# Experts' silu written with Tanh, the router's sigmoid with Exp and a reciprocal

## The chip, the cores and the metric

The kernel runs on one core of a Trainium2 chip. The metric is the device time of one execution in microseconds (us); several runs are made and their median is compared. The core has TensorE (PE, matmuls; its weight loads are shown as PEld), VectorE (DVE), ScalarE (ACT), GpSimd (POOL) and SyncE (SP, which issues the DMAs). Every engine runs its own instructions in order and waits for the others by semaphores.

## What is computed

A decoder of two layers: six sublayers in a row on 512 tokens of width 256, each followed by a residual addition and a layer norm. The change lies in the sixth, a mixture of 64 experts with a shared expert:

```python
N, TOPK, E, CAP, H, HS = 512, 6, 64, 128, 32, 64
y_s, g_s = split(x @ w_shared_up)                    # 512 x 64 each
shared = (silu(g_s) * y_s) @ w_shared_down
scores = sigmoid(x @ w_gate)                         # 512 x 64
topk_idx = top_k(scores, 6)
w = scores at topk_idx, divided by their sum
# an expert takes at most CAP tokens: valid = position in its list < CAP
g_r, v_r = split(x @ w_up[e])                        # for each expert, 32 each
out_r = (silu(g_r) * v_r) @ w_down[e]
x = layernorm(x + shared + sum over the 6 experts of w * valid * out_r)
```

## The kernel before

The program has six stages, one for each sublayer; each engine's part of stage n is a function `stageN` in that engine's block, with the instructions and the semaphores written out by hand. No scheduler reorders them: what is written is the order on the engine.

Stage 6 doesn't gather tokens by expert. It computes every expert for all 512 tokens and multiplies by a gate that is zero where the expert wasn't chosen. Four experts make a group, so that the hidden units of a group fill 128 partitions, and the 512 tokens lie along the free dimension; there are 16 groups, g = 0 to 15. All data here are float32.

On TensorE (L1124 to L1179): the router's matmuls go to PSUM bank 7. `up(g)` multiplies the tokens by the two halves of a group's up weights, into bank g % 2 (the half that goes through silu) and bank 2 + g % 2; it waits until `gate(g-2)` on VectorE has read these banks. `down(g)` multiplies `hidden` of a group by its down weights and adds to the output in banks 6 and 7. The order is: router, `up(0)` to `up(3)`, the count of tokens per expert (L1148), `up(4)`, the transposes of the gates (L1154), the shared expert's up matmul, `up(5)`, then `down(0)`, the shared expert's down matmuls (L1177), `up(6)`, `down(1)`, `up(7)` and so on to `down(9)`, `up(15)`, and `down(10)` to `down(15)` without anything between them. The matmuls of `up` have line L762, those of `down` L1162.

On ScalarE (L728 to L747): the sigmoid of the router's scores (L730), the silu of each group (`silu_of`, L737) from PSUM to SBUF, a copy of the transposed gates (L742), the silu of the shared expert (L745).

On VectorE (L1577 to L1625): top 8 and their indices (L1581, L1584), the one-hot counts of each of four blocks of tokens (L1596 to L1598), with `gate(0)` behind the first block and `gate(1)` behind the third, then `gate(2)`, `gate(3)`, the capacity test (L1608), `gate(4)`, the shared expert's product (L1611), `gate(5)`, and the loop. `gate(g)` (L1593) multiplies silu by the other half of `up`, from PSUM to the SBUF tile `gated`; `hidden` (L1622) multiplies `gated` by the rows of gates that a DMA has spread over the partitions. In the loop each `hidden(g)` is followed by `gate(g+5)` while there are groups left, so `gate(15)` stands between `hidden(10)` and `hidden(11)`. `link` makes the engine wait for the end of the instruction that it is given before the next one begins.

Of the kernel before, what the change touches and what calls it, by code (L numbers as in the profile page):

```python
# [17 lines left out]
ACT = mybir.ActivationFunctionType  # L18
# [12 lines left out]
N = B * S  # L31
TT = N // P
# [14 lines left out]
E1, HE, HS, TOPK, CAP = 64, 32, 64, 6, 128  # L47
# [18 lines left out]
def build(nc, t, out):  # L66

    with ExitStack() as ctx:
# [5 lines left out]
        def sem(name):  # L74
            if name not in sems:
                sems[name] = ctx.enter_context(nc.semaphore(name))
            return sems[name]
# [3 lines left out]
        def bank(k, n=1):  # L81
            return ps[:, 512 * k:512 * (k + n)]
# [48 lines left out]
        def carve(where, at, shape, dt=F32, rows=P):  # L131

            words = math.prod(shape) * mybir.dt.size(dt) // 4
            assert at + words <= area[where].shape[1], (where, at, shape)
            v = area[where][0:rows, at:at + words]
            if dt != F32:
                v = v.bitcast(dt)
            if len(shape) == 2:
                v = v.rearrange("p (a b) -> p a b", a=shape[0])
            if len(shape) == 3:  # L140
                v = v.rearrange("p (a b c) -> p a b c", a=shape[0], b=shape[1])
            return v

        def tiny(shape, dt=F32):
            v = carve("small", taken["small"], shape, dt)
            taken["small"] += (math.prod(shape) * mybir.dt.size(dt) + 3) // 4
            return v
# [88 lines left out]
        gate1T = carve("b", 0, [N], rows=E1)  # L236
        silu = carve("b", N, [2, N])
# [5 lines left out]
        score1 = carve("b", 8 * N, [TT, E1])  # L243
# [4 lines left out]

        base = 8 * N + 4 * TT * E1 + TOPK * E1
        silu_shared = carve("b", base + N, [N], rows=HS)  # L250
        top1, idx1, idx1f = tiny([TT, 8]), tiny([TT, 8], U32), tiny([TT, 8])
        sum1, rsum1 = tiny([TT]), tiny([TT])

# [58 lines left out]
        def linker(eng, name):  # L312

            count = [0]

            def link(ins):
                count[0] += 1
                ins.then_inc(sem(name), 1)
                eng.wait_ge(sem(name), count[0])
            return link  # L320
# [245 lines left out]
        def _(act):  # L566
            link = linker(act, "act_chain")
# [159 lines left out]

            def stage6():  # L728
                act.wait_ge(sem("score1_ps"), 1)
                act.activation(score1.rearrange("p i e -> p (i e)"), bank(7)[:, 0:TT * E1], ACT.Sigmoid).then_inc(sem("score1_ready"), 1)  # L730

                def silu_of(g):
                    act.wait_ge(sem("up_ps"), g + 1)
                    if g >= 2:

                        act.wait_ge(sem("gated_ready"), g - 1)
                    act.activation(silu[:, g % 2, :], bank(g % 2), ACT.Silu).then_inc(sem("silu_ready"), 1)  # L737

                for g in range(4):
                    silu_of(g)  # L740
                act.wait_ge(sem("gate1T_ps"), 1)
                act.activation(gate1T, bank(5)[0:E1, :], ACT.Copy).then_inc(sem("gate1T_ready"), 1)  # L742
                silu_of(4)
                act.wait_ge(sem("shared_ps"), 1)
                act.activation(silu_shared, bank(4)[HS:2 * HS, :], ACT.Silu).then_inc(sem("silu_shared_ready"), 1)  # L745
                for g in range(5, NG):
                    silu_of(g)  # L747

# [441 lines left out]
        def _(dve):  # L1190
            link = linker(dve, "dve_chain")
            TS, TTN, STT = dve.tensor_scalar, dve.tensor_tensor, dve.scalar_tensor_tensor
# [61 lines left out]
            for c in range(DC):  # L1254
# [10 lines left out]
                if c:  # L1265
# [4 lines left out]
                    op1=ALU.add).then_inc(sem("phi_ready"), 1)  # L1270
# [305 lines left out]

            def stage6():  # L1577
                dve.wait_ge(sem("score1_ready"), 1)
                ids = iota_row[:, 0:E1].unsqueeze(1).broadcast_to([P, TOPK, E1])
                for i in range(TT):  # L1580
                    last = dve.max(top1[:, i, :], score1[:, i, :])  # L1581
                link(last)
                for i in range(TT):
                    last = dve.max_index(idx1[:, i, :], top1[:, i, :], score1[:, i, :])  # L1584
                link(last)
                link(dve.tensor_copy(idx1f, idx1))
                link(dve.tensor_reduce(sum1, top1[:, :, 0:TOPK], AX.X, ALU.add))
                link(dve.reciprocal(rsum1, sum1))

                def gate(g):  # L1590

                    dve.wait_ge(sem("silu_ready"), g + 1)
                    TTN(out=gated[:, g % AHEAD, :], in0=bank(2 + g % 2), in1=silu[:, g % 2, :], op=ALU.mult).then_inc(sem("gated_ready"), 1)  # L1593

                for i in range(TT):
                    link(TTN(out=hot, in0=idx1f[:, i, 0:TOPK].unsqueeze(2).broadcast_to([P, TOPK, E1]), in1=ids, op=ALU.is_equal))  # L1596
                    link(dve.tensor_reduce(picked[:, i, :], hot.rearrange("p k e -> p e k"), AX.X, ALU.add))
                    dve.tensor_copy(picked_b[:, i, :], picked[:, i, :]).then_inc(sem("picked_ready"), 1)  # L1598
                    if i % 2 == 0:
                        gate(i // 2)  # L1600
                link(TTN(out=gate1, in0=picked, in1=score1, op=ALU.mult))
                link(TTN(out=gate1, in0=gate1, in1=rsum1.unsqueeze(2).broadcast_to([P, TT, E1]), op=ALU.mult))
                gate(2)
                gate(3)
                dve.wait_ge(sem("count_ps"), 1)

                flat = gate1.rearrange("p i e -> p (i e)")
                STT(out=flat, in0=bank(6)[:, 0:TT * E1], scalar=float(CAP), in1=flat, op0=ALU.is_le, op1=ALU.mult).then_inc(sem("gate1_ready"), 1)  # L1608
                gate(4)
                dve.wait_ge(sem("silu_shared_ready"), 1)  # L1610
                TTN(out=shared, in0=bank(4)[0:HS, :], in1=silu_shared, op=ALU.mult).then_inc(sem("shared_ready"), 1)  # L1611
                gate(5)
                dve.wait_ge(sem("gated_ready"), AHEAD)
                for g in range(NG):
                    s = g % 2
                    if g >= AHEAD:
                        dve.wait_ge(sem("gated_ready"), g + 1)
                    if g >= 2:

                        dve.wait_ge(sem("hidden_used"), g - 1)  # L1620
                    dve.wait_ge(sem(f"gate_rows_{g % 4}"), 16 * (g // 4 + 1))
                    TTN(out=hidden[:, s, :], in0=gate_rows[:, g % 4, :], in1=gated[:, g % AHEAD, :], op=ALU.mult).then_inc(sem("hidden_ready"), 1)  # L1622
                    if g and g - 1 + AHEAD < NG:
                        dve.wait_ge(sem("hidden_ready"), g)
                        gate(g - 1 + AHEAD)  # L1625
# [52 lines left out]
```

## Time and profile before

| | before |
|---|---|
| time, median of 3 runs | 472.29 us (471.53 to 473.58) |
| span of the profiled execution | 473.8 us |
| TensorE busy | 388.1 us, 82% of the span |
| VectorE busy | 303.7 us, 64% |
| ScalarE busy | 215.5 us, 45% |
| GpSimd busy | 118.4 us, 25% |
| chain of waits, share of the span | TensorE 53%, VectorE 15%, DMA 12%, ScalarE 10% |

The span goes from the first to the last instruction of one execution that was profiled; that execution's time apart from its span isn't given, and the span is 1.5 us above the median of the three runs, which were timed without a profile. The busy shares are means over the six stages, of which only the last, from about 369 us on, is touched by the change. The chain of waits is followed back from the last instruction: at each step to what released it.

### The profile page before, as it was taken

The page shows a single profiled execution, that of the slowest core. Times are in us where ns is not written, and L with a number is a line of the kernel's source. Part 1 is how long each engine was busy: PE and PEld are TensorE (multiplying, and loading weights), DVE is VectorE, ACT ScalarE, POOL GpSimd, SP SyncE. Part 2 cuts the span into 40 slices and gives each one's busy share as a digit, 9 for nine tenths or more (in the row PEclk, how much of TensorE's full clock was granted, in tenths as well). Part 3 has the DMA queues.
Part 4 walks back from the last instruction along what each step waited for, and adds up shares of the span by engine and source line. Part 5 has one row for each costly group of instructions (what it writes and reads, how often), then busy time and mean ns, then how long its engine had stood idle before and what let it go on. Part 6 is the DMA issues. An engine that isn't in the chain of part 4 may idle for free.

```text
span 473.8 us, 6810 instructions
## 1 busy us (share of the span) xinstructions
PE 388.1 (82%) x2387; PEld 225.7 (48%) x2387; DVE 303.7 (64%) x611; ACT 215.5 (45%) x551; POOL 118.4 (25%) x215
## 2 busy tenths in 40 slices
PE   5996969389987999999754867768676998999993
PEld 2645457244434566576532223333344544665572
DVE  4984498959624697878646979989871362132235
ACT  2664221272235765855214789899881311111100
POOL 8248646828460000000080111212110000000002
PEclk9989895779988899999985589998975698999997
DMA  8992110670000000000000999999982004011211
GB/s 244 318 361 25 1 2 1 223 310 1 0 1 0 1 3 0 2 1 1 2 0 13 265 169 172 155 163 173 131 162 51 0 0 143 24 44 49 63 44 44
DMA packets 75521, 39.84 MB, mean 84 GB/s; under 512 B 64160, under 2 KB 71264, under 8 KB 75040
## 3 DMA queue, kind: packets, MB, share of 16 engines
q1 hardware_dynamic: 73184, 39.35, 34.1%
q0 software_dynamic: 2304, 0.07, 1.4%
q8 instruction: 19, 0.31, 0.3%
q14 instruction: 14, 0.11, 0.1%
HBM read 21.58 MB, written 2.88 MB: 52 GB/s over the span
## 4 chain that ended last, share of the span: by engine, by line
PE 53%; DVE 15%; DMA 12%; ACT 10%; issue 5%; POOL 4%; SPq 0%; POOLq 0%; ACTq 0%; DVEq 0%
PE ps L762 27%; ACT area_b L692 7%; PE ps L1162 6%; DMA area_b<-area_b 6%; PE ps L945 5%; PE ps L956 5%; PE ps L975 3%; DMA area_a<-area_b 3%; POOL deltas L490 2%; PE ps L939 2%; DMA area_b<-deltas 1%; DVE area_a L1275 1%; DMA deltas<-entry_w,small 1%; ACT area_a L673 1%; DVE stats L1282 1%
## 5 line engine op out<-in xcount | busy, mean ns | idle before, releaser
L1535 DVE CUSTOM_DVE_ANT_0 area_a<-ps,zero,small 128x1024 f32<-128x1024 f32 x64 | 79.4, 1278 | 9.7 <-ACT area_b L692 5.0
L692 ACT ACTIVATE area_b<-area_a,small 128x1024 int16<-128x1024 f32 x64 | 73.0, 1142 | 11.3 <-DMA area_b<-area_b 5.9
L673 ACT ACTIVATE area_a<-ps,small 128x256 f32<-128x256 f32 (+1 forms) x128 | 51.9, 432 | 31.0 <-DVE small L1426 28.7
L459 POOL TENSOR_SCALAR var_eps<-meanvar 128x1 f32<-128x1 f32 x24 | 6.6, 273 | 225.3 <-DVE meanvar L1283 225.2
L762 PE MATMUL ps<-xT_odd,early 128*128 128x512 f32 x128 | 59.5, 613 | 0.0
L1054 PE MATMUL ps<-area_b 128*128 128x512 bf16 x128 | 45.0, 446 | 13.5 <-DVE small L1535 12.4
L1593 DVE TENSOR_TENSOR area_b<-ps,area_b 128x512 f32<-128x512 f32 x16 | 11.1, 691 | 55.7 <-ACT area_b L737 55.7
L1426 DVE TENSOR_REDUCE small<-ps 128x4 f32<-128x1024 f32 (+1 forms) x24 | 29.3, 1222 | 18.3 <-PE ps L945 18.1
L737 ACT ACTIVATE area_b<-ps 128x512 f32<-128x512 f32 x16 | 9.5, 596 | 67.2 <-PE ps L762 67.2
L762 PE MATMUL ps<-area_b,xT_even 128*128 128x512 f32 x64 | 31.1, 631 | 9.0 <-ACT area_b L650 9.0
L762 PEld LDWEIGHTS ps<-xT_odd,early 128*128 128x128 f32 x128 | 25.0, 197 | 27.1 <-issue 26.6
L547 POOL TENSOR_SCALAR small<-small 128x1 f32<-128x1 f32 x64 | 12.5, 195 | 87.5 <-DVE small L1535 87.5
L1162 PE MATMUL ps<-area_a,area_b 128*128 128x256 f32 x128 | 31.0, 392 | 2.6 <-DVE area_b L1622 2.6
L1435 DVE COPY area_b<-ps 128x512 f32<-128x512 f32 x48 | 30.8, 681 | 1.0 <-PE ps L956 0.9
L1162 PEld LDWEIGHTS ps<-area_a,area_b 128*128 128x128 f32 x128 | 24.8, 195 | 11.5 <-issue 7.8
L490 POOL DMA_INDIRECT deltas<-entry_w,small x16 | 26.0, 1624 | 10.6 <-DMA deltas<-entry_w,small 3.8
L945 PE MATMUL ps<-area_a,area_b 32*128 32x256 f32 (+1 forms) x160 | 28.1, 460 | 0.0
L956 PE MATMUL ps<-ident,area_a 128*128 128x128 f32 x192 | 27.2, 286 | 1.0 <-DVE area_b L1435 1.0
L673 ACT ACTIVATION_READ_ACCUMULATOR area_a<-ps,small 128x1 f32 x128 | 27.9, 218 | 0.0
L956 PEld LDWEIGHTS ps<-ident,area_a 128*128 128x128 f32 x192 | 21.3, 144 | 12.2 <-ACT area_a L673 8.5
L1054 PEld LDWEIGHTS ps<-area_b 128*128 128x128 bf16 x128 | 8.2, 102 | 34.3 <-DVE small L1535 28.6
L762 PEld LDWEIGHTS ps<-area_b,xT_even 128*128 128x128 f32 x64 | 12.3, 203 | 22.0 <-issue 22.0
(265 smaller groups left out, 667.4 us busy)
## 6 DMA issues: line engine op xcount, KB each, us to landing
early<-in_w_up_dram SPq DMA_DIRECT2D x1, 4096.0 KB, 16.1
area_b<-gates_out SPq DMA_DIRECT2D x16, 256.0 KB, 3.0
deltas<-area_b SPq DMA_DIRECT2D x1, 2112.0 KB, 17.8
area_b<-deltas SPq DMA_DIRECT2D x2, 1024.0 KB, 5.9
area_a<-in_w_down_dram SPq DMA_DIRECT2D x1, 2048.0 KB, 8.5
early<-in_ctxT_dram SPq DMA_DIRECT2D x1, 1024.0 KB, 13.1
early<-in_ctx_dram SPq DMA_DIRECT2D x1, 1024.0 KB, 14.0
early<-in_w_qkv_dram SPq DMA_DIRECT2D x2, 384.0 KB, 5.1
```

The costliest lines, as they stand in the source:

```text
L490: pool.indirect_dma_start(out=deltas, out_offset=bass.IndirectOffsetOnAxis(ap=place[:, j:j + 1], axis=0), in_=entry_w[:, j, :], in_offset= ...
L673: a = act.activation(p1[:, n % 2, x * nk * P:(x + 1) * nk * P], scores1(n)[:, x * nk * P:(x + 1) * nk * P], ACT.Exp, bias=nmx1[:, n % 2, x ...
L692: act.activation(px[:, u % PX, :], sx[:, u % 3, :], ACT.Exp, bias=nbx[:, u:u + 1], accum_out=zx[:, i, h:h + 1]).then_inc(sem("px_ready"), 1)
L762: mm = pe.matmul(dst, lhsT(c), rhs(c), start=start and c == 0, stop=stop and c == DC - 1, **kw)
L945: mm = pe.matmul(dst, qT1[rows, c, i * P:(i + 1) * P], kT1[rows, c, heads, kt * P:(kt + 1) * P], start=False, stop=b == nk - 1)
L956: mm = pe.transpose(bank(4 + x)[:, y * P:(y + 1) * P], p1[:, n % 2, (4 * x + y) * P:(4 * x + y + 1) * P], ident[:])
L975: mm = pe.matmul(bank(6)[g * HU * DH1:(g + 1) * HU * DH1, c * P:(c + 1) * P], v1[:, (kt * (H1 // HU) + c * UC + g) * HU + j, :], pT1[:, n ...
L1054: mm = pe.matmul(bank(2 * (u % 2) + half), qTx[:, h // 2, h % 2, i * P:(i + 1) * P], kTx[:, h // 2, half * 512:(half + 1) * 512], start=Tr ...
L1162: mm = pe.matmul(proj(i), hidden[:, g % 2, i * P:(i + 1) * P], w_down[:, g, :], start=g == 0 and i % 2 == 0, stop=g == NG - 1, skip_group_ ...
L1426: dve.tensor_reduce(nmx1[:, n % 2, 0:8 // nk], scores1(n).rearrange("p (h k) -> p h k", k=nk * P), AX.X, ALU.max, negate=True).then_inc(se ...
L1435: dve.tensor_copy(pT1[:, n % 4, 4 * x * P:4 * (x + 1) * P], bank(4 + x)).then_inc(sem("pT1_ready"), 1)
L1535: dve.tensor_tensor_reduce(sx[:, u % 3, :], bank(2 * (u % 2), 2), zero[:].broadcast_to([P, B * M]), qsc[:, i, h:h + 1], LOWEST, ALU.add, A ...
```

## The change

Silu is written as x/2 * (1 + tanh(x/2)): ScalarE computes tanh(x/2) in place of silu, a new scalar_tensor_tensor on VectorE makes (tanh + 1) * x, reading x from PSUM, and the product with the other half follows as before, linked behind it. The factor 1/2 of the groups goes into the copy of the transposed gates. For the shared expert, whose x stands in other partitions than the product, ScalarE makes a copy of x/2 as well, in a new tile `half_shared`. The router's sigmoid becomes 1 / (1 + exp(-x)): Exp on ScalarE, an addition and a reciprocal on VectorE.

```diff
+        half_shared = carve("b", base + 2 * N, [N], rows=HS)
...
             def stage6():            # ScalarE
                 act.wait_ge(sem("score1_ps"), 1)
-                act.activation(score1.rearrange("p i e -> p (i e)"), bank(7)[:, 0:TT * E1], ACT.Sigmoid).then_inc(sem("score1_ready"), 1)
+                act.activation(score1.rearrange("p i e -> p (i e)"), bank(7)[:, 0:TT * E1], ACT.Exp, scale=-1.0).then_inc(sem("score1_ready"), 1)
...
-                    act.activation(silu[:, g % 2, :], bank(g % 2), ACT.Silu).then_inc(sem("silu_ready"), 1)
+                    act.activation(silu[:, g % 2, :], bank(g % 2), ACT.Tanh, scale=0.5).then_inc(sem("silu_ready"), 1)
...
-                act.activation(gate1T, bank(5)[0:E1, :], ACT.Copy).then_inc(sem("gate1T_ready"), 1)
+                act.activation(gate1T, bank(5)[0:E1, :], ACT.Copy, scale=0.5).then_inc(sem("gate1T_ready"), 1)
...
-                act.activation(silu_shared, bank(4)[HS:2 * HS, :], ACT.Silu).then_inc(sem("silu_shared_ready"), 1)
+                act.activation(silu_shared, bank(4)[HS:2 * HS, :], ACT.Tanh, scale=0.5)
+                act.activation(half_shared, bank(4)[HS:2 * HS, :], ACT.Copy, scale=0.5).then_inc(sem("silu_shared_ready"), 1)
...
             def stage6():            # VectorE
                 dve.wait_ge(sem("score1_ready"), 1)
+                link(TS(score1, score1, 1.0, None, ALU.add))
+                link(dve.reciprocal(score1, score1))
...
                     dve.wait_ge(sem("silu_ready"), g + 1)
+                    link(STT(out=silu[:, g % 2, :], in0=silu[:, g % 2, :], scalar=1.0, in1=bank(g % 2), op0=ALU.add, op1=ALU.mult))
                     TTN(out=gated[:, g % AHEAD, :], in0=bank(2 + g % 2), in1=silu[:, g % 2, :], op=ALU.mult).then_inc(sem("gated_ready"), 1)
...
                 dve.wait_ge(sem("silu_shared_ready"), 1)
+                link(STT(out=silu_shared, in0=silu_shared, scalar=1.0, in1=half_shared, op0=ALU.add, op1=ALU.mult))
                 TTN(out=shared, in0=bank(4)[0:HS, :], in1=silu_shared, op=ALU.mult).then_inc(sem("shared_ready"), 1)
```

What the diff doesn't show is that the program loads ScalarE's function tables where a function needs another set. On ScalarE, at the beginning of stage 6, this stood in the program before (`area_b` is the memory in which the tiles of this stage lie, `ps` is PSUM):

```order
L622 ACTIVATE xT_odd<-ps 128x2x128 x4
L730 ACT_TABLE_LOAD
L730 ACTIVATE area_b<-ps 128x256
L737 ACT_TABLE_LOAD
L737 ACTIVATE area_b<-ps 128x512 x4
L742 ACTIVATE area_b<-ps 64x512
```

and this stands there now, one line further down in the file:

```order
L623 ACTIVATE xT_odd<-ps 128x2x128 x4
L731 ACTIVATE area_b<-ps 128x256
L738 ACTIVATE area_b<-ps 128x512 x4
L743 ACTIVATE area_b<-ps 64x512
L738 ACTIVATE area_b<-ps 128x512
L746 ACTIVATE area_b<-ps 64x512
L747 ACTIVATE area_b<-ps 64x512
```

Both loads of stage 6 are gone; the one that is left stands at the beginning of the program, as it did before.

On VectorE, from the capacity test to the first `gate` of the loop, this stood before:

```order
L1608 SCALAR_TENSOR_TENSOR area_b<-ps,area_b 128x256
L1593 TENSOR_TENSOR area_b<-ps,area_b 128x512
L1611 TENSOR_TENSOR area_b<-ps,area_b 64x512
L1593 TENSOR_TENSOR area_b<-ps,area_b 128x512
L1622 TENSOR_TENSOR area_b<-area_b 128x512 x2
```

and this stands there now (L1597 is the new operation, L1598 the product of `gate`, L1628 `hidden`):

```order
L1613 SCALAR_TENSOR_TENSOR area_b<-ps,area_b 128x256
L1597 SCALAR_TENSOR_TENSOR area_b<-area_b,ps 128x512
L1598 TENSOR_TENSOR area_b<-ps,area_b 128x512
L1616 SCALAR_TENSOR_TENSOR area_b<-area_b 64x512
L1617 TENSOR_TENSOR area_b<-ps,area_b 64x512
L1597 SCALAR_TENSOR_TENSOR area_b<-area_b,ps 128x512
L1598 TENSOR_TENSOR area_b<-ps,area_b 128x512
L1628 TENSOR_TENSOR area_b<-area_b 128x512 x2
```

Each `gate` has one operation more, and `hidden(0)`, the first of the last row, stands behind both operations of `gate(5)`. On the other engines the program is the same.

## Rows read from the trace of the kernel before

**Rows 1.** The first line of the profile's page.

```profile
span 473.8 us, 6810 instructions
```

**Rows 2.** Chain of waits in stage 6: start us, length us, what.

```profile
392.26 5.17 PE ps L762 x12
...
455.24 1.74 PE ps L1162 x8
```

**Rows 3.** Stretches: length, busy us of PE, PEld, DVE, ACT, POOL; clock; DMA.

```profile
369.00:397.40 28.40, 28.40 (x81) 14.06 (x80) 13.14 (x36) 7.16 (x11) 0.00 (x0) 0.87 0.05 11
...
405.10:457.00 51.90, 51.86 (x161) 30.31 (x160) 12.63 (x20) 5.97 (x10) 0.00 (x0) 1.00 0.16 46
```

**Rows 4.** Timeline of TensorE, `down(0)`: start, length, engine, line [idle before, releaser].

```profile
399.64 3.21 PE L1162 MATMUL ps<-area_a,area_b 128*128 128x256 f32 x8 [2.23 <-DVE area_b L1622]
```

**Rows 5.** Timeline of VectorE and TensorE at the last `gate`.

```profile
455.97 0.69 DVE L1593 TENSOR_TENSOR area_b<-ps,area_b 128x512 f32<-128x512 f32 x1 [3.87 <-ACT area_b L737]
456.58 1.28 DVE L1622 TENSOR_TENSOR area_b<-area_b 128x512 f32<-128x512 f32 x2
...
457.32 8.90 PE L1162 MATMUL ps<-area_a,area_b 128*128 128x256 f32 x40 [0.35 <-DVE area_b L1622]
```

**Rows 6.** VectorE by line and form: count | busy us, mean ns | idle before.

```profile
L1275 DVE RECIPROCAL area_a<-area_a 128x512 f32<-128x512 f32 x2 | 6.7, 3352 | 0.1
...
L1216 DVE RECIPROCAL area_b<-area_b 128x128 f32<-128x128 f32 x1 | 1.0, 953 | 0.0
...
L1273 DVE TENSOR_SCALAR area_a<-area_a 128x512 f32<-128x512 f32 x2 | 0.9, 426 | 0.1
...
L1608 DVE SCALAR_TENSOR_TENSOR area_b<-ps,area_b 128x256 f32<-128x256 f32 x1 | 0.4, 412 | 0.0
...
L1215 DVE TENSOR_SCALAR area_b<-area_b 128x128 f32<-128x128 f32 x1 | 0.2, 220 | 0.0
```

**Rows 7.** Timeline of VectorE, `gate(0)` to `hidden(0)`.

```profile
378.38 0.69 DVE L1593 TENSOR_TENSOR area_b<-ps,area_b 128x512 f32<-128x512 f32 x1 [2.06 <-ACT area_b L737]
...
382.07 0.68 DVE L1593 TENSOR_TENSOR area_b<-ps,area_b 128x512 f32<-128x512 f32 x1
...
385.31 0.69 DVE L1593 TENSOR_TENSOR area_b<-ps,area_b 128x512 f32<-128x512 f32 x1 [0.23 <-ACT area_b L737]
388.68 0.69 DVE L1593 TENSOR_TENSOR area_b<-ps,area_b 128x512 f32<-128x512 f32 x1 [2.67 <-ACT area_b L737]
...
398.07 0.69 DVE L1593 TENSOR_TENSOR area_b<-ps,area_b 128x512 f32<-128x512 f32 x1 [2.75 <-ACT area_b L737]
398.80 1.29 DVE L1622 TENSOR_TENSOR area_b<-area_b 128x512 f32<-128x512 f32 x2
```

**Rows 8.** Stretches of TensorE alone: length, busy us, granted clock, DMA share, GB/s.

```profile
226.00:235.00 9.00, 6.46 (x95) 1.00 0.01 3
325.00:328.00 3.00, 1.62 (x20) 1.00 0.80 148
328.00:331.00 3.00, 2.71 (x20) 0.59 1.02 193
397.00:400.00 3.00, 0.77 (x3) 1.00 0.94 307
400.00:403.00 3.00, 3.00 (x9) 0.53 0.49 179
```

**Rows 9.** Timeline of weight loads: the first of `up(3)` and of `up(4)`.

```profile
383.99 0.19 PEld L762 LDWEIGHTS ps<-xT_odd,early 128*128 128x128 f32 x1 [0.24 <-issue]
...
388.11 0.30 PEld L762 LDWEIGHTS ps<-xT_odd,early 128*128 128x128 f32 x2
```

**Rows 10.** Timeline of ScalarE at the beginning of stage 6.

```profile
369.17 1.28 ACT L730 ACT_TABLE_LOAD   x1
372.08 0.38 ACT L730 ACTIVATE area_b<-ps 128x256 f32<-128x256 f32 x1 [1.62 <-PE ps L762]
...
377.75 0.60 ACT L737 ACTIVATE area_b<-ps 128x512 f32<-128x512 f32 x1 [3.99 <-PE ps L762]
```

## The prediction

> **What bounds the kernel now.** I read the chain of waits first, for the part of the program that the change touches: stage 6, the experts, which begins near 369 us of a span of 473.8 us [rows 1]. The chain runs through TensorE nearly everywhere there: matmuls of `up` to 397.4 us (392.26 + 5.17), and `down(10)` to 456.98 us (455.24 + 1.74) [rows 2]. The table of stretches says the same: from 369 to 397.4 TensorE is busy 28.40 us of 28.40, from 405.1 to 457 it is busy 51.86 of 51.90, while VectorE works 13.14 and 12.63 us in these stretches [rows 3]. So VectorE has much room on average, and an operation added to it costs nothing where TensorE has other work. The question is only at which places TensorE waits for VectorE, and at which it comes to.
>
> The waits of TensorE in this stage are two. `down(0)` at 399.64 starts after 2.23 us of idleness, released by VectorE's L1622 (`hidden`) [rows 4]: TensorE has done `up(0)` to `up(5)` and has nothing else until `hidden(0)` exists. And `down(11)` at 457.32 starts after 0.35 us, again released by L1622 [rows 5]: there are no more `up` blocks to fill the time. Between these, in the loop, VectorE waits 3.87 us for ScalarE before each `gate` [rows 5], so an operation of under a microsecond disappears.
>
> **The change, step by step.**
>
> *One operation more in each `gate`.* Its operands are 128x512 float32, one in PSUM. No row of before has just this form. The nearest are the `gate` product itself, L1593, 0.69 us, which also reads PSUM at this size [rows 7], and the scalar_tensor_tensor L1608 that reads PSUM at 128x256, 412 ns [rows 6]. I take 0.69 us, the row of the same size. The product behind it now waits for a semaphore of its own engine; a linked pair shows some 0.04 us between end and start (398.07 + 0.69 = 398.76, next start 398.80 [rows 7]). So a `gate` grows by 0.73 us. Bounds: 0.41, if the width cost nothing beyond the 256 row, and 0.86, twice that row and the gap.
>
> *Before `down(0)`.* `gate(5)` starts at 398.07 after 2.75 us of waiting for ScalarE, and `hidden(0)` at 398.80 stands right behind it [rows 7]. Tanh and silu are both one pass of ScalarE, so 398.07 stays. `hidden(0)` moves to 399.53, `down(0)` to 400.37: **0.73 us on the path**. The clock enters here. In 397 to 400 the granted clock is 1.00, in 400 to 403 it is 0.53 [rows 8], that is 2.4 and then 1.2 GHz, after the idle 2.23 us. The 0.36 us and a little more that TensorE did at full clock before the fall would now be done after it. If the rise comes when it came before, the term is about 0.6; if the rise comes as much later, it is about 1.0. I keep 0.73.
>
> *The tail.* `gate(15)` starts at 455.97, and `hidden(11)` at 456.58 queues behind it on VectorE although it doesn't need its result; `down(11)` waits for `hidden(11)` [rows 5]. So another **0.73 us on the path**, and TensorE's idle time grows from 0.35 to 1.08 us.
>
> *The ten `gate`s between them* (`gate(6)` to `gate(14)`, and `gate(4)`, which stands before the shared expert) cost nothing: the cover is the 3.87 us of VectorE's waiting per group, with 3.1 left. Were that cover gone, each group would cost 0.73, some 7 us in all. The shared expert's ScalarE copy (0.6 us, as a 512-wide pass of Silu [rows 10]) and its VectorE operation stand in the 2.75 us ahead of `gate(5)`.
>
> *The router's add and reciprocal*, 128x256, on VectorE ahead of everything else in stage 6. Reciprocals: 953 ns at width 128 and 3352 at 512 [rows 6], a straight line of 6.25 ns an element, so 1.75 us at 256. The add: 220 ns at 128 and 426 at 512 [rows 6], so 0.29. With two links, 2.1 us. Behind them queue the top-8 search, the index search and the first one-hot count. Their cover is the 2.06 us that VectorE idles before `gate(0)` at 378.38 [rows 7]: just enough, so `gate(0)` starts as before. If that cover were gone, they would cost up to 2.1 us.
>
> *`gate(0)` to `gate(3)`, the start.* From here VectorE has no idle time until `gate(2)`. `gate(1)`, at 382.07 before, starts 0.73 later and ends at 384.21 (382.80 + 0.73 + 0.68). `up(3)` writes the banks that `gate(1)` reads; its first weights were loaded at 383.99, with 0.24 us of slack ahead of each load [rows 7, 9]. With the 0.06 us that a semaphore took from `hidden(11)` to `down(11)` (456.58 + 0.68 to 457.32 [rows 5]) the load comes at 384.27, 0.28 late, of which the slack takes 0.24: 0.04 us. `gate(2)`, at 385.31 after 0.23 idle, is pushed by 1.46 - 0.23 = 1.23 and ends at 387.96; `up(4)`'s weights were loaded at 388.11 [rows 7, 9]: in time by a tenth. `gate(3)` waited 2.67 us before 388.68 [rows 7], so there VectorE is back in step; the capacity test L1608 behind it comes 0.73 later, at about 390.5, and the transposes that wait for it follow the eight matmuls of `up(4)`, which end near 391.5 (388.11 and 8 x 0.43). Start: **0.05 us**; bounds 0 (all within the slack) and 0.3 (add at the 512-wide price, three more links).
>
> *Two table loads fewer.* ScalarE's loads for Sigmoid and Silu, 1.28 us each (two; one stands in the rows), are gone. After the first ScalarE still waited 1.62 us for TensorE, before the first Silu 3.99 us [rows 10]. So nothing is gained: ScalarE only waits longer. If these waits were not there, they would be worth 2.57.
>
> **Sum.** 0.73 + 0.73 + 0.05 = 1.51 us; by the bounds 0.8 (two waits of 0.41) to 2.3 (1.0, 0.86 and 0.3, with rounding). The profiled execution spans 473.8 us, already 1.5 above the median of the runs, 472.29, and 0.2 above their highest, so it was one of the slower ones; a profile of the changed kernel should span about 475.3, and its runs have a median of 472.29 + 1.51 = **473.8 us**. 0.5% of 472.29 is 2.4 us, about what a measurement of this kernel can tell from no change; the forecast lies under that.
>
> **The rivals.**
>
> *The clock falls in the tail (slower).* TensorE's idle time between `down(10)` and `down(11)` becomes 1.08 us. Idle time of that order is where the granted clock sometimes falls: in 325 to 328 TensorE was busy 1.62 of 3.00 us, and the clock went from 1.00 there to 0.59 in 328 to 331 [rows 8]. Against it: in 226 to 235 it was busy 6.46 of 9.00, and the clock stayed at 1.00 throughout [rows 8]. [...] The price, from the fall at 400: a stretch of 3.4 us or so at half clock (0.53 over 400 to 403), of which half is lost, 1.7 us. Then 1.5 + 1.7 = 3.2, 475.5 us. Chance 0.11.
>
> *VectorE becomes the bound of the start (slower).* The cover before `gate(0)` is used up to 0.05 us, and `up(3)` has a slack of 0.24. Anything that the router's two operations cost beyond 2.1 us goes to the path. With a reciprocal at the 512-wide price, 3.35, it is 1.6 more: 475.4 us; the decisive point is 1 us more, at 474.8. The two measured widths lie on both sides of the new one, so 0.05.
>
> *Only one wait counts.* The longer idle time ahead of `down(0)` costs nothing, because the stretch at the low clock that follows ends at the same time and the work after the rise catches up. Then 0.8 us, 473.1. Against it: TensorE is busy without a break from 405.1, so nothing is there to catch up with. 0.07.
>
> *The table loads were paid for (faster).* If the switch of tables cost TensorE or VectorE something that the idle times hide, the change gives back 2.57 us and takes 1.51: 471.2 us. What speaks against it is that TensorE's first `up` blocks run straight through 369 to 397.4, whatever ScalarE does. 0.04. The Trainium skill (ScalarE: Activation LUTs, What ACT_TABLE_LOAD costs) speaks for it: it puts a switch of sets at 1283 ns for the load and 1380 ns for draining the engine, 2.66 us in all, and advises calling activations by set, as the changed kernel does. This trace agrees on the load (1.28), and has a draining time in no row: what stands behind the first load, 1.62 us, is ended by TensorE. By that figure two switches would be an estimated 5.3 us, and the sum 468.5.
>
> **How the numbers follow.** The forecast has 0.73, the clock 0.11, the start 0.05, one wait 0.07, the tables 0.04. The predicted time is the forecast's. Its own range, 473.1 to 474.6, with the spread of a median of a few runs (they lie between 471.53 and 473.58) is 472.7 to 475.0; to hold 8 in 10 with cases beyond it, I extend it upward to the clock's case: 472.7 to 475.7. Slower by over 0.5% (above 474.65): the clock 0.11, the start 0.04, the upper edge of the forecast 0.04, together 0.19. Faster by over 0.5%: half of the tables' case and a little for the spread, 0.03. The rest, 0.78, is within 0.5%.
>
> **What would show it.** In the changed profile: the new operation near 0.69 us and the reciprocal near 1.75; `gate(0)`'s first operation at about 378.4; TensorE without idle time up to 397.4; its wait before `down(0)` near 3.0 and before `down(11)` near 1.1, with the granted clock at 1.00 after the latter; no table load in stage 6, and ScalarE waiting for TensorE as before. It is wrong if TensorE waits before `up(2)`, `up(3)` or `up(4)` for more than 0.3 us, if a wait shows up inside the loop, or if the clock falls after 457.

## The result: slower, and by more than forecast

| | before | after |
|---|---|---|
| median, 4 runs each | 472.45 us (471.53 to 473.58) | 477.67 us (476.67 to 479.94) |
| ratio, 95% interval | | 1.0117 (1.0079 to 1.0155) |
| span of the profiled execution | 473.8 us | 476.2 us |
| once more, on one chip: median | 475.36 us (29 runs, 468.19 to 479.19) | 478.26 us (12 runs, 472.29 to 483.97) |
| ratio, 95% interval | | 1.0076 (1.0012 to 1.0139) |

The forecast was 473.8 us in a range of 472.7 to 475.7. The first measurement is above the range, 5.2 us over before. The second, with more runs, is over before by 2.9 us (medians) or 3.6 us (ratio) and shows how far runs of one program lie apart: 11 us for the kernel before. (The ratios are formed without the runs that lie more than 1.5% above the fastest of their kernel, in the second measurement 17 of the 29 before and 3 of the 12 after; the medians are those of all runs.) So the first part of the question is what stage 6 really costs, and the second what the rest of the 5.2 is.

Stage 6 in the profile after. First VectorE's timeline, from the router to the gates (the lines of the file are one to six further down; L1597 is the new operation in `gate`, L1598 the product, L1628 `hidden`); these answer to [rows 5, 7].

```profile
375.09 0.29 DVE L1581 TENSOR_SCALAR area_b<-area_b 128x256 f32<-128x256 f32 x1 [4.50 <-ACT area_b L731]
375.42 1.75 DVE L1582 RECIPROCAL area_b<-area_b 128x256 f32<-128x256 f32 x1
...
380.96 0.68 DVE L1597 SCALAR_TENSOR_TENSOR area_b<-area_b,ps 128x512 f32<-128x512 f32 x1
381.68 0.69 DVE L1598 TENSOR_TENSOR area_b<-ps,area_b 128x512 f32<-128x512 f32 x1
...
386.08 0.69 DVE L1598 TENSOR_TENSOR area_b<-ps,area_b 128x512 f32<-128x512 f32 x1
...
400.59 0.69 DVE L1597 SCALAR_TENSOR_TENSOR area_b<-area_b,ps 128x512 f32<-128x512 f32 x1 [1.55 <-ACT area_b L738]
401.31 0.69 DVE L1598 TENSOR_TENSOR area_b<-ps,area_b 128x512 f32<-128x512 f32 x1
402.03 1.29 DVE L1628 TENSOR_TENSOR area_b<-area_b 128x512 f32<-128x512 f32 x2
```

The prices came as worked out: 0.29 for the add, 1.75 for the reciprocal, 0.68 to 0.69 for the new operation, 0.72 from its start to that of the product. `gate(0)` at 380.96 follows VectorE's work without idle time: the 2.06 us that stood before it [rows 7] are used up, and it starts 10.79 us after the last norm product of stage 5, as before (10.80). TensorE's timeline of the same kernel:

```profile
374.43 12.24 PE L764 MATMUL ps<-xT_odd,early 128*128 128x512 f32 x24
386.82 3.70 PE L764 MATMUL ps<-xT_odd,early 128*128 128x512 f32 x8 [0.16 <-DVE area_b L1598]
...
402.87 1.97 PE L1164 MATMUL ps<-area_a,area_b 128*128 128x256 f32 x8 [2.95 <-DVE area_b L1628]
...
459.63 8.90 PE L1164 MATMUL ps<-area_a,area_b 128*128 128x256 f32 x40 [1.08 <-DVE area_b L1628]
```

The two waits grew as forecast, from 2.23 to 2.95 us [rows 4] and from 0.35 to 1.08 [rows 5], and a new one of 0.16 stands before `up(3)`. None of the waits that the prediction named as signs of being wrong is there: nothing over 0.3 us before `up(2)` to `up(4)`, and nothing inside the loop. ScalarE, with no table load, only waits longer than in [rows 10]:

```profile
374.67 0.38 ACT L731 ACTIVATE area_b<-ps 128x256 f32<-128x256 f32 x1 [2.92 <-PE ps L764]
379.84 0.60 ACT L738 ACTIVATE area_b<-ps 128x512 f32<-128x512 f32 x1 [4.78 <-PE ps L764]
```

And the granted clock of TensorE (stretches: length, busy, clock, DMA):

```profile
370.00:374.00 4.00, 3.36 (x16) 0.50 0.00 0
374.00:378.00 4.00, 4.00 (x8) 0.51 0.00 0
400.00:404.00 4.00, 1.13 (x5) 1.00 0.75 228
404.00:408.00 4.00, 4.00 (x15) 1.00 0.44 131
459.00:467.00 8.00, 7.37 (x34) 1.00 0.12 33
```

Stage 6 began at 1.2 GHz, and after the 2.95 us of idle time the clock did *not* fall, though it fell after 2.23 in the profile before [rows 8]. So the two spans, 473.8 and 476.2, can't be compared directly. For what follows each profile has four numbers: the length of stage 6 (from the start of the last norm product of stage 5 to that of stage 6, 367.58 and 471.28 before, 370.17 and 473.60 after); what the low clock took of it (TensorE's busy time by its granted clock's shortfall from 1.00, added up over quarters of a microsecond); the rest; and TensorE's idle time in it.

The runs x1 to x12 are described below; "filled" ones have extra matmuls that keep TensorE busy ahead of stage 6.

| profile | stage 6 | low clock | rest | TensorE idle |
|---|---|---|---|---|
| before | 103.70 | 5.84 | 97.86 | 8.12 |
| x1 before again | 98.06 | 0.00 | 98.06 | 8.11 |
| after | 103.43 | 3.62 | 99.81 | 9.71 |
| x2 after again | 103.43 | 3.60 | 99.83 | 9.74 |
| x3 functions only | 99.74 | 1.71 | 98.04 | 8.12 |
| x4 VectorE only | 103.43 | 3.24 | 100.19 | 10.10 |
| x5 filled, before | 99.70 | 1.71 | 97.99 | 8.11 |
| x6 filled, after | 103.24 | 1.66 | 101.58 | 11.14 |
| x7 after, Sigmoid | 99.50 | 0.00 | 99.50 | 9.56 |
| x8 after, hidden early | 100.93 | 4.02 | 96.91 | 7.34 |
| x9 filled, after, Sigmoid | 99.51 | 0.00 | 99.51 | 9.57 |
| x10 filled, router only | 98.71 | 0.00 | 98.71 | 8.25 |
| x11 filled, before, hidden early | 96.90 | 0.00 | 96.90 | 7.22 |
| x12 after, Sigmoid, again | 102.59 | 3.12 | 99.47 | 9.56 |

### The profile page after: what moved, and what is told of

The parts are those of the page before. It is cut to its first block and busy times, and to the rows that moved or that the text cites. A ratio compares the mean times of both kernels' runs of the same rounds, so it can differ in the third digit from the quotient of the medians.

```text
span 476.2 us, 6805 instructions
## 1 busy us (share of the span) xinstructions
PE 379.4 (80%) x2364; PEld 222.5 (47%) x2387; DVE 317.3 (67%) x630; ACT 213.3 (45%) x550; POOL 117.7 (25%) x215
## 5 line engine op out<-in xcount | busy, mean ns | idle before, releaser
L1056 PE MATMUL ps<-area_b 128*128 128x512 bf16 x116 | 41.2, 441 | 16.1 <-DVE small L1537 13.3
L1597 DVE SCALAR_TENSOR_TENSOR area_b<-area_b,ps 128x512 f32<-128x512 f32 x16 | 11.0, 686 | 41.3 <-ACT area_b L738 41.3
L1164 PE MATMUL ps<-area_a,area_b 128*128 128x256 f32 x128 | 29.8, 380 | 4.0 <-DVE area_b L1628 4.0
L947 PE MATMUL ps<-area_a,area_b 32*128 32x256 f32 (+1 forms) x160 | 29.3, 477 | 0.0
```

Source lines behind the costliest of these rows:

```text
L947: mm = pe.matmul(dst, qT1[rows, c, i * P:(i + 1) * P], kT1[rows, c, heads, kt * P:(kt + 1) * P], start=False, stop=b == nk - 1)
L1056: mm = pe.matmul(bank(2 * (u % 2) + half), qTx[:, h // 2, h % 2, i * P:(i + 1) * P], kTx[:, h // 2, half * 512:(half + 1) * 512], start=Tr ...
L1164: mm = pe.matmul(proj(i), hidden[:, g % 2, i * P:(i + 1) * P], w_down[:, g, :], start=g == 0 and i % 2 == 0, stop=g == NG - 1, skip_group_ ...
```

## The experiments

Ratios are to runs of the kernel before on the same chip. There were three such groups of 29 runs, one for x1 to x4, one for x5 to x8 and one for x9 to x12; their medians are 475.36, 475.05 and 474.80 us.

### Which part costs: functions or VectorE

x1 and x2 are the two kernels unchanged.

> The kernel before, unchanged, to have the spans and granted clocks of its own runs beside its times, and a second profile. If the profiled execution of before was an outlier (its span of 473.8 us lies above the time of every run), the spans here lie near 470.7, which is 472.4 less the 1.7 that lie between span and time in the runs of the changed kernel. If before has less around its span than the changed kernel has, the spans lie at 472 and above, and part of the 5.2 us stands outside the program's work. Ratio to before 1.000 in either case.

Measured: 473.94 us, ratio 0.9991 (0.9932 to 1.005). The profiled execution spans 469.0 and took 470.79, so some 1.8 us lie around the span here too. The span of the first profile, 473.8, then belongs to an execution of about 475.6 (an estimate), which is high beside the first four runs and ordinary beside the 29. None of the 5.2 us stands outside the span.

> The changed kernel, unchanged, on the same chip as the next two. Theory V (VectorE's new operations delay TensorE at two places and the rest of the 5.2 us is the spread of few runs): 1.5 to 2.5 us over before, ratio 1.003 to 1.005. Theory F (the functions or their tables cost something that stands in no wait of stage 6) and theory C (the longer idle times of TensorE make its clock fall more often): about 5 us, ratio 1.011.

Measured: ratio 1.0076 (1.0012 to 1.0139); its profile repeats that of the first within 0.03 us in every column of the table. The interval holds V's 1.003 to 1.005 as well as the 1.011 of F and C.

x3 takes VectorE's new operations out:

```diff
-                link(TS(score1, score1, 1.0, None, ALU.add))
-                link(dve.reciprocal(score1, score1))
...
-                    link(STT(out=silu[:, g % 2, :], ... in1=bank(g % 2), ...))
...
-                link(STT(out=silu_shared, ...))
```

> ScalarE as in the changed kernel (Exp, Tanh, the second pass of the shared expert, no table load in stage 6), VectorE as before: the factor x of silu, the add and the reciprocal are left out, so the experts' values and the choice of experts are others. V and C: no change, within 0.5 us of before, since ScalarE waits for TensorE at all these places. F: 3.5 us or more over before.

Measured: ratio 1.0003 (0.9948 to 1.0058); rest 98.04, idle 8.12, against 98.06 and 8.11 in x1. Theory F falls, since its 1.011 lies outside the interval: the functions, the second pass for the shared expert and the two table loads are worth nothing that stage 6 shows, in either direction.

x4 is the opposite, the kernel before with the operations on a spare tile:

```diff
+        spare = carve("b", 15 * N, [N])
...
+                link(TS(spare[:, 0:TT * E1], flat1, 1.0, None, ALU.add))
+                link(dve.reciprocal(spare[:, 0:TT * E1], spare[:, 0:TT * E1]))
...
+                    link(STT(out=spare, in0=silu[:, g % 2, :], scalar=1.0, in1=bank(g % 2), op0=ALU.add, op1=ALU.mult))
...
```

> ScalarE as before (Sigmoid, Silu, with their table loads), VectorE with every operation that the change adds (add, reciprocal, 17 scalar_tensor_tensors, each linked), their results written to a spare tile that nobody reads. V: 1.5 us over before, ratio 1.003, TensorE idle about 2.95 us before down(0) and 1.08 before down(11) in the profile. C: about 5 us, ratio 1.011, with more falls of the clock in stage 6. F: 1.5 us.

Measured: 477.15 us, ratio 1.0105 (1.0028 to 1.0183), with 2.95 and 1.08 us of idle time at the two places, and 0.53 before `up(3)` where the profile after has 0.16:

```profile
382.64 3.70 PE L763 MATMUL ps<-xT_odd,early 128*128 128x512 f32 x8 [0.53 <-DVE area_b L1598]
```

So the waits that the change adds to stage 6 are VectorE's. The time by itself doesn't tell V from C, whose 1.003 and 1.011 both lie in the interval. In the profiles theory C finds no support: with 2.23 us before `down(0)` the clock fell there in two of five profiles (before and x5; not in x1, x3, x10), with 2.95 in two of seven (x6 and x12; not in after, x2, x4, x7, x9).

The three profiles after, x2 and x4 have stage 6 at 103.43 us to the hundredth, whatever the low clock took. What it took and the wait before `up(3)` add up to the same: 3.62 + 0.16, 3.60 + 0.18 and 3.24 + 0.53. That is what a stage looks like whose start another engine paces, and the reason for the next theory, S.

### Does the start depend on the clock?

In the profile before, stage 6 began at 1.2 GHz; TensorE's timeline, and a stretch with its granted clock:

```profile
371.83 16.18 PE L762 MATMUL ps<-xT_odd,early 128*128 128x512 f32 x32
```

```profile
372.00:376.00 4.00, 4.00 (x6) 0.50 0.00 0
```

In x1 it began at the high clock. VectorE's and TensorE's timeline of x1, and the same stretch:

```profile
375.26 0.68 DVE L1593 TENSOR_TENSOR area_b<-ps,area_b 128x512 f32<-128x512 f32 x1
...
378.95 0.69 DVE L1593 TENSOR_TENSOR area_b<-ps,area_b 128x512 f32<-128x512 f32 x1
```

```profile
370.89 13.95 PE L762 MATMUL ps<-xT_odd,early 128*128 128x512 f32 x32
```

```profile
372.00:376.00 4.00, 4.00 (x10) 1.00 0.00 0
```

`up(0)` to `up(3)` took 13.95 us in place of 16.18, and `gate(0)` at 375.26 has no idle time before it, in the kernel *before* the change. The 2.06 us in [rows 7] were TensorE's slowness, not VectorE's room. To have the high clock in every profile, x5 and x6 fill TensorE's idle time at the end of stage 5 with matmuls into a free bank, which nobody reads (12 and 5 before the last two `apply`, 3, 1, 2 and 3 behind them):

```diff
+            def fill(count):
+                for _ in range(count):
+                    pe.matmul(bank(0), ident_b[:], window[:, 0, :], start=True, stop=True)
...
+                    if u == units:
+                        pe.wait_ge(sem("maxx_ready"), units)
+                        fill(12)
+                    if u == units + 2:
+                        fill(5)
...
```

> The kernel before, with 26 matmuls whose results nobody reads put into TensorE's idle time at the end of stage 5, so that its clock is high when stage 6 begins. Stage 6 (from the start of the last norm product of stage 5 to that of stage 6) took 103.7 us in the first profile of before, which began it at the low clock, and 98.1 in the second, which began it at the high one. Both theories expect about 98 here, if the clock doesn't fall before down(0), where TensorE idles 2.23 us; the whole is 2 to 5 us faster than before, unless the added matmuls delay stage 5.

Measured: 470.76 us, ratio 0.9949 (0.9906 to 0.9992): faster than before, by 2.4 us (ratio) or 4.3 (medians). Rest 97.99. The clock did fall at `down(0)`, at a cost of 1.7, which is all of this profile's low clock.

> The changed kernel with the same 26 matmuls. Theory S (the cover of the router's add and reciprocal is TensorE's slow start: with the high clock up(0) and up(1) end earlier, VectorE sets the pace from the router's scores to up(4), and TensorE waits before up(2) and up(3)): stage 6 takes 3.2 to 3.7 us more than with x5, about 101.5, with 1.5 to 2.2 us of idle time of TensorE before up(2) and up(3) together, beside the 2.95 and 1.08 before down(0) and down(11). Theory V alone (the price is 1.5 us whatever the clock): 99.6, and less than 0.3 us idle before up(2) and up(3).

Measured: 475.41 us, ratio 1.0037 (0.999 to 1.0083), over x5 by 4.2 us (ratios) or 4.65 (medians); rest 101.58, 3.59 more than x5. TensorE's timeline of x6, and its clock in the stretches at the start:

```profile
370.54 7.08 PE L764 MATMUL ps<-xT_odd,early 128*128 128x512 f32 x16
378.48 3.70 PE L764 MATMUL ps<-xT_odd,early 128*128 128x512 f32 x8 [0.86 <-DVE area_b L1613]
382.88 3.70 PE L764 MATMUL ps<-xT_odd,early 128*128 128x512 f32 x8 [0.70 <-DVE area_b L1613]
```

```profile
368.00:372.00 4.00, 3.47 (x22) 1.00 0.00 0
372.00:376.00 4.00, 4.00 (x11) 1.00 0.00 0
```

`up(2)` and `up(3)` now wait for the products of `gate(0)` and `gate(1)`, 0.86 and 0.70. The four `up` blocks end at 386.58 (382.88 + 3.70), 16.04 us after they began, against 13.95 in x1: 2.1 us at the start, and 2 x 0.72 at the other two places, make 3.5 of the 3.59. S holds: its 3.2 to 3.7 came out, and V's 0.3 us or less of waiting did not.

### Which operations make VectorE late

x7 gives the router its Sigmoid back; x9 is x7 with the filling matmuls; x10 has the router's operations alone, with the filling matmuls.

```diff
-                act.activation(score1..., ACT.Exp, scale=-1.0).then_inc(sem("score1_ready"), 1)
+                act.activation(score1..., ACT.Sigmoid).then_inc(sem("score1_ready"), 1)
...
-                link(TS(score1, score1, 1.0, None, ALU.add))
-                link(dve.reciprocal(score1, score1))
```

> The changed kernel with the router as before: Sigmoid on ScalarE, no add and no reciprocal on VectorE; silu stays with Tanh. S: VectorE comes 2.1 us earlier to gate(0), so TensorE doesn't wait before up(2) and up(3) at either clock, or by 0.1 us; the price over before is 1.46 us, that is 1 to 2 us less than the changed kernel, ratio to before 1.003. V: the same as the changed kernel within 0.2 us.

Measured: 479.68 us from six runs, ratio 1.0152 (1.0073 to 1.0231); rest 99.50, at the high clock. Profile and time disagree, hence x12:

> x7 once more, because its six runs (472 to 484 us, mean 479.3) lie above what its profile shows for stage 6 (99.5 us, the price of 1.46 over the second profile of before). If its runs scatter as those of the other kernels do, the mean is 1.5 us over before, 476; if something that its stage 6 doesn't show costs it 3 us, it is near 479 again.

Measured: 476.46 us, ratio 1.0074 (1.0023 to 1.0125); rest 99.47. The second sample lies 3.2 us under the first, so the first says little of the kernel, and the second came out as expected of runs that scatter. What stage 6 of it costs is the same in both profiles, 1.4 over x1 and x3 (98.06 and 98.04).

> x7 (Tanh and VectorE's operation in each gate, the router with Sigmoid as before) with the 26 filling matmuls of x5 and x6, so that stage 6 begins at the high clock. By S, the router's add and reciprocal are what makes VectorE late at the start: without them TensorE waits before up(2) and up(3) by 0.3 us at most, its stage 6 takes 1.5 us more than that of x5 at equal clock (99.5 after taking off what the low clock costs), and the time lies 1.5 us over x5 and 2 us under x6. If the operation in gate(0) and gate(1) alone were enough to make VectorE late, it would lie near x6.

Measured: 470.93 us, ratio 0.9974 (0.9931 to 1.0016); rest 99.51, which is 1.52 over x5 and 2.07 under x6, as S has it. TensorE's timeline of x9:

```profile
369.89 13.95 PE L764 MATMUL ps<-xT_odd,early 128*128 128x512 f32 x32
...
396.19 1.96 PE L1179 MATMUL ps<-area_a,area_b 128*128 128x256 f32 x8 [2.95 <-DVE area_b L1641]
```

No wait at the start, 13.95 as in x1, although `gate(0)` and `gate(1)` are 0.72 longer each.

> The kernel before with the 26 filling matmuls and the router's add and reciprocal alone, written to a spare tile that nobody reads; silu and the gates as before. By the second profile of before, gate(0) ended 1.4 us ahead of the first weight load of up(2) at the high clock, and gate(1) 1.5 us ahead of that of up(3): so 2.1 us more cost 0.5 to 0.7 us before up(2), and nothing or little more before up(3), 98.5 to 98.7 after taking off the low clock, against 98.0 in x5. At the low clock of the first profile the same operations would cost nothing. If the two parts simply added up, it would be x6 less x9, 2.1.

Measured: 469.32 us, ratio 0.9922 (0.9884 to 0.9961), which can't be told from x5; in the profile rest 98.71, 0.72 more than x5. TensorE's timeline of x10:

```profile
368.55 14.61 PE L763 MATMUL ps<-xT_odd,early 128*128 128x512 f32 x32
```

The four blocks take 0.66 more than in x1. So at the high clock the router's two operations cost 0.7 alone and 2.1 with the longer gates, while the longer gates alone cost nothing there: they share one cover, of about 1.4 us in x1, where `gate(0)` ends at 375.94 (375.26 + 0.68) and the first weights of `up(2)` are loaded at

```profile
377.39 0.19 PEld L762 LDWEIGHTS ps<-xT_odd,early 128*128 128x128 f32 x1 [0.24 <-issue]
```

What one of them takes of it, the other lacks.

### Taking the gates out of the way

`hidden(0)` and `hidden(11)` wait behind a `gate` whose result they don't need. x8 is the changed kernel with `hidden(0)` and `hidden(1)` before `gate(5)` and each later `hidden` one place earlier:

```diff
-                gate(5)
-                dve.wait_ge(sem("gated_ready"), AHEAD)
...
+                hide(0)
+                hide(1)
+                for g in range(5, NG):
+                    if g >= AHEAD:
+                        hide(g - 4)
+                        dve.wait_ge(sem("hidden_ready"), g - 5)
+                    gate(g)
+                for g in range(NG - 4, NG):
+                    hide(g)
...
```

> The changed kernel with VectorE's order changed: hidden(0) and hidden(1) before gate(5), and each later hidden(g) before gate(g+4) in place of behind it, so that down(0) and down(11) wait for no gate. All theories: TensorE's wait before down(0) falls from 2.95 us to what the DMA of the gates' rows needs, 1.0 to 1.6 us, the one before down(11) from 1.08 to nothing; 2.4 to 3 us less than the changed kernel, about 0.5 to 1 us under before by V, and 1 us over it by S, since the waits at the start stay.

Measured: 473.46 us, ratio 1.0007 (0.9962 to 1.0051); rest 96.91, 2.9 less than after. The granted clock at the start of x8, and TensorE's timeline:

```profile
374.00:378.00 4.00, 4.00 (x8) 0.50 0.00 0
```

```profile
374.54 16.09 PE L764 MATMUL ps<-xT_odd,early 128*128 128x512 f32 x32
...
401.82 1.97 PE L1164 MATMUL ps<-area_a,area_b 128*128 128x256 f32 x8 [1.79 <-DVE area_b L1626]
...
455.61 10.52 PE L1164 MATMUL ps<-area_a,area_b 128*128 128x256 f32 x48
```

The last six `down` run in one piece (48 matmuls), and the wait before `down(0)` is 1.79. The order of VectorE's work gives back what the change took. The expectation had the waits at the start stay, which by S would have left x8 1 us over before; here the low clock took 4.02 us, more than the 3.77 to 3.78 that low clock and wait make together in after, x2 and x4, and no wait is left at the start. So this order of the changed kernel is shown at the low clock alone. At the high clock no run has it; by x6, 2.1 us at the start would remain (an estimate).

> The version that the runs so far point to: the kernel before (Silu, Sigmoid) with the filling matmuls and with hidden ahead of gate in VectorE's order, as in x8. TensorE waits 1.5 to 1.8 us before down(0) in place of 2.23, by x8's 1.79, and not at all before down(11): 0.8 us less than x5, 4.3 us less than before, ratio 0.991.

Measured: 466.62 us, ratio 0.9889 (0.9837 to 0.9941), under before on that chip by 5.3 us (ratio) or 8.2 (medians): the fastest kernel here. The rest is 96.90, 1.1 less than x5, so the order is worth something without the change as well; the wait before `down(0)` is 1.69.

## Why the prediction was wrong

- **VectorE's new operation, before `down(0)` and in the tail (0.73 each).** Right: 0.72 or 0.73 at each place, in every profile that has it in the order of the changed kernel. The loop between hides the other ten, as said.
- **The clock in the tail (0.11) and after `down(0)`.** With 1.07 or 1.08 us idle before `down(11)` the clock stayed at 1.00 to the end of the matmuls in all seven profiles that have it. Nor did the clock fall more often after `down(0)` with the longer wait (two of seven) than with the shorter (two of five).
- **The table loads.** No gain, as worked out: x3 is 1.0003. The 2.66 us for a switch that the Trainium skill gives (ScalarE: Activation LUTs, What ACT_TABLE_LOAD costs) is a price on ScalarE, and would stand here in time that ScalarE waits anyway; no run shows it on the path.
- **The router's add and reciprocal, and the start (0.05).** This is the step that failed. "Their cover is the 2.06 us that VectorE idles before `gate(0)` at 378.38 [rows 7]: just enough." The durations were right to 0.01 us; the cover was not VectorE's to give. It came from `up(0)` beginning at 1.2 GHz in the one profile that was read, and was put into the sum as if it were always there. At the low clock of that profile the 0.05 would hold: its low clock took some 4.1 us at the start (5.84 less 1.7 at `down(0)`, an estimate), about what it took in x8, where no wait is left. Elsewhere TensorE's wait at the start is 0.16 (after) to 0.53 us (x4) at the low clock, and the start costs 2.1 at the high one (x6), so the price of the change in stage 6 is 1.5 to 2.0 or 3.6. The rival that VectorE becomes the bound of the start was there with 0.05, but by a dearer reciprocal; the mechanism that acts is an earlier TensorE. The row that gave it away was quoted: clock 0.87 in 369 to 397.4 [rows 3].
- **The base and the range.** By the medians this is the larger part of the miss. 1.51 was added to 472.29, the median of three runs that lie within 2.1 us, and the range was drawn with that spread. The same kernel's later runs lie between 468 and 479, with medians of 474.8 to 475.4 in three groups of 29. The 477.67 is 2.3 to 2.9 us above those, which a price of 1.5 to 3.6 in stage 6 accounts for. By these medians the remaining 2.3 to 2.9 of the first 5.2 is a low base. By the ratios the change costs 5.5 us in the first measurement and 3.6 in the second (0.6 to 6.6), so the rest is 1.9. The first four runs of before have no spans beside their times, and why they lie so close together and so low isn't settled. In the profile after, stage 6 has 1.6 us more of waits than before, close to the forecast of 1.51: the start can explain up to 2.1 us of the miss, but hardly any of it in this execution.
- **The upper bound.** Its terms, 1.0, 0.86 and 0.3, add up to 2.16 and not 2.3; the measured time lies above the range either way.

What stays open is how the low and the high start mix in the average. Of the nine profiles without filling matmuls five began stage 6 wholly at 1.2 GHz (before, after, x2, x4, x8), two partly (x3, x12) and two at 2.4 GHz (x1, x7). Among them all four with the whole of the changed kernel's work on VectorE (after, x2, x4, x8) began at the low clock; the price of 3.6 at the high one is seen with the filling matmuls only. By the nine profiles the mean price is an estimated 2 us or a little more, which lies in the interval of x2, 0.6 to 6.6 us, and is not measured by it more closely.

## What to carry to other kernels

An idle time in front of an operation is room for more work only if it would be there at the other clock of TensorE too: look at the granted clock of the stretch, and work out the start once with the matmuls at full speed. When two added pieces of work use one cover, cost them together: at the high clock the longer gates alone were free and the router's operations cost 0.7, both together 2.1. And where an engine waits behind an operation whose result it doesn't need, the order is worth more than the operation: moving `hidden` ahead of `gate` gave 2.9 us in the changed kernel, 2.2 of it in the two waits where the new operation had cost 1.45, and 1.1 us in the kernel before.

## What was not expected of the hardware

Keeping TensorE busy with 26 matmuls that nobody reads, before a stage that begins after a stretch of waiting, made the kernel faster by 2.4 us (x5, ratio 0.9949) or 4.3 (medians). And the same idle time does not always cost the clock: after 2.23 us before `down(0)` it fell in two profiles of five, after 2.95 in two of seven.
